# Sigmoid attention: the score slots of two pairs of heads take turns

## The reference, cut to what matters

```
x_h = layernorm(x).reshape(B, T, H, HD)                # B=2, T=1024, H=16, HD=8
Q, K, V = (x_h * sign(bv_q), x_h * sign(bv_k), x_h * sign(bv_v))
scores = einsum('bqhd,bkhd->bhqk', Q, K) * HD ** -0.5
attn = where(causal, sigmoid(scores * 4.0), 0.0)
out = einsum('bhqk,bkhd->bqhd', attn, V)
```

## Time and profile before

| what | us |
| --- | --- |
| runs: median (lowest to highest) | 1137.98 (1134.75 to 1138.6) |
| the profiled execution, its own time | 1134.96 |
| its span in the trace | 1133.0 |
| sigmoid stage in it, first score matmul to first matmul of the experts | 36.84 to 196.44 |

### The profile page before, as it was taken

How to read it: one execution, slowest core, us unless ns; L and a number is a source line. 1 busy time by engine, 2 the same in 40 slices (tenths; PEclk the granted TensorE clock), 3 DMA queues, 4 the chain that set the end, 5 groups by cost and what they waited for, 6 DMA issues and landing times. The chain is left out here.

```text
span 1133.0 us, 22305 instructions
## 1 busy us (share of the span) xinstructions
PE 1026.2 (91%) x7828; PEld 641.8 (57%) x7828; DVE 757.1 (67%) x1707; ACT 728.0 (64%) x1087; POOL 541.2 (48%) x707
## 2 busy tenths in 40 slices
PE   3899999999999469999999899999999878999997
PEld 2444444777776334555554445555444556878785
DVE  7235341777865476887788788777785257676766
ACT  1699987555546137777777677777776555545453
POOL 1377775665644122333455533344222276655564
PEclk9999999999999658999999999999999899999999
DMA  4541231536466596888888888888771574343342
GB/s 161 190 128 62 84 98 55 160 115 189 140 179 198 192 254 195 243 241 240 244 260 254 235 245 240 240 245 240 217 220 40 128 226 121 122 118 121 118 122 92
DMA packets 146430, 197.41 MB, mean 174 GB/s; under 512 B 33292, under 2 KB 113149, under 8 KB 146285
## 3 DMA queue, kind: packets, MB, share of 16 engines
q1 hardware_dynamic: 126254, 184.32, 52.4%
q0 software_dynamic: 20064, 11.66, 6.1%
HBM read 123.00 MB, written 72.74 MB: 173 GB/s over the span
## 5 line engine op out<-in xcount | busy, mean ns | idle before, releaser
L1090 DVE TENSOR_REDUCE a_part<-a_duo 128x2 f32<-128x1024 f32 (+3 forms) x256 | 215.3, 855 | 14.1 <-PE a_duo L963 12.6
L755 POOL DMA_DIRECT2D scr_y1c<-ys x240 | 118.9, 504 | 204.1 <-DVE ys L1071 201.2
L1083 DVE CUSTOM_DVE_ANT_0 a_band_sum<-a_duo,a_rel_raw 128x256 f32<-128x256 f32 (+2 forms) x320 | 131.4, 447 | 84.2 <-PE a_duo L963 64.3
L1529 POOL TENSOR_TENSOR f_hid_lo<-f_hid,att 128x512 fp32r<-128x512 f32 (+1 forms) x100 | 129.4, 1297 | 106.8 <-ACT att L1498 106.8
L976 PE MATMUL a_duo<-att 32*128 32x512 f32 (+3 forms) x672 | 139.2, 410 | 21.1 <-DVE a_part L1090 12.9
L963 PE MATMUL a_duo<-att 31*128 31x512 f32 (+3 forms) x672 | 145.4, 428 | 9.0 <-DVE a_part L1090 4.1
L706 ACT ACTIVATE a_probs<-a_duo 128x1024 f32<-128x1024 f32 x192 | 139.9, 829 | 14.1 <-PE a_duo L655 12.7
L1043 ACT ACTIVATE a_rel<-a_rel_ps 128x384 f32<-128x384 f32 x240 | 117.5, 490 | 48.3 <-PE a_rel_ps L950 47.7
L1661 DVE TENSOR_TENSOR f_hid<-f_u,w_share 128x512 f32<-128x512 f32 (+1 forms) x168 | 116.3, 692 | 27.5 <-POOL f_hid_lo L1529 4.6
L644 POOL TENSOR_TENSOR a_probs<-a_probs,const 128x256 f32<-128x256 f32 x128 | 101.5, 809 | 48.8 <-ACT a_probs L706 48.6
L1529 POOL TENSOR_TENSOR f_hid_lo<-f_hid,f_hid_hi 128x512 fp32r<-128x512 f32 x68 | 88.0, 1294 | 76.0 <-ACT f_hid_hi L1498 76.0
(11 more groups left out here) (268 smaller groups left out, 2048.1 us busy)
## 6 DMA issues: line engine op xcount, KB each, us to landing
a_rel_raw<-scr_rel SPq DMA_DIRECT2D x128, 384.0 KB, 4.5
scr_rel<-a_rel SPq DMA_DIRECT2D x120, 384.0 KB, 3.7
w_share<-scr_cw SPq DMA_DIRECT2D x144, 128.0 KB, 3.2
w_share<-scr_cw SPq DMA_DIRECT2D x44, 256.0 KB, 3.3
scr_y1c<-ys POOLq DMA_DIRECT2D x240, 8.0 KB, 3.7
w_share<-scr_cw SPq DMA_DIRECT2D x20, 192.0 KB, 2.8
w_share<-scr_cw SPq DMA_DIRECT2D x16, 224.0 KB, 3.0
att<-scr_q SPq DMA_DIRECT2D x36, 96.0 KB
```

The costliest lines, as they stand in the source:

```text
L755: eng.dma_start(scr["y1c"][w, b, head, :, at:at + T // 4], sb["ys"][32 * (2 * hd + c) + HD * w:32 * (2 * hd + c) + HD * (w + 1), h % 2, :] ...
L1083: ins = dve.tensor_tensor_reduce(band_sum[:, m % 2, hd, 0:wide], both[:, hd, (a - 4 * x) * P:(b - 4 * x) * P], rel_raw[:, e % RING, hd, (a ...
L1090: ins = dve.tensor_reduce(part[:, h % 2, x, :, j % 4], both[:, :, lo * P:hi * P], AX.X, ALU.max, negate=True)
L1529: pool.tensor_tensor(hid_lo[0:m, n % 4, :], hid[0:m, n % 2, :], f32(hid_hi[0:m, n % 4, :]), ALU.subtract).then_inc(lo_ready, 1)
```

## The change

- Two pairs of heads form a quad of 24 slots. Even slots belong to the even pair, in the order before (`EVEN`); odd slots belong to the odd pair, which goes through its lower half first (`ODD`).
- Each pair sums in a bank of its own: `acc_of(h)` is `acc[pair % 2]` for both halves. The four groups of a quad end after slots 8, 15, 23 and 24 (`ENDS`), in the order odd pair lower, even pair upper, even pair lower, odd pair upper (`GROUPS`). The first slot of a group waits for the save of the last group in its bank, `before(h)`.
- `vs` has four places in place of two, `probs` seven in place of eight (`KEPT`).
- The loads of pair 1 move from SyncE's queue at the start of the stage to ScalarE's in `prepare`, ahead of its Exp. SyncE loads the next quad's two pairs behind the third and behind the fourth group of a quad.

```
--- before.py
+++ after.py
@@ -411,6 +411,9 @@
             for c in range(NC):
                 act.wait_ge(turned, c + 1)
                 act.activation(x_hi[:, c * CH:(c + 1) * CH], bank[c][:], ACT.Copy).then_inc(hi_ready, 1)
+            act.wait_ge(ahead.qk_stored, 16 * 6)
+            for hd in range(2):
+                load_sigmoid_head(sb, scr, act, 1, hd, ahead.qk_loaded[1])
             act.wait_ge(exp_in, 1)
             act.activation(sc[:], sc[:], ACT.Exp).then_inc(exp_ready, 1)
 
@@ -515,12 +518,15 @@
     HALF, QUARTER = T // 2, T // 4
     PAIRS = B * H // 2
     K3 = TERMS * HD
-    PER = 12
-    SLOTS = PER * PAIRS
-    KEPT = 8
+    PER = 24
+    SLOTS = PER * PAIRS // 2
+    KEPT = 7
     HELD, LAG = 7, 4
     TURN, STEP = 20, 6 * P
     UPPER, LOWER = (0, 7, 1, 6, 2, 5, 3, 4), (0, 3, 1, 2)
+    EVEN, ODD = [(1, kt) for kt in UPPER] + [(0, kt) for kt in LOWER], [(0, kt) for kt in LOWER] + [(1, kt) for kt in UPPER]
+    GROUPS = ((1, 0), (0, 1), (0, 0), (1, 1))
+    ENDS = (8, 15, 23, 24)
     with ExitStack() as ctx:
         def tile(name, shape, dt=F32):
             return ctx.enter_context(nc.sbuf_tensor("a0_" + name, shape, dt))
@@ -529,7 +535,7 @@
             return ctx.enter_context(nc.semaphore("a0_" + name))
 
         qs, ks = (sb["att"][:, i, :, :] for i in range(2))
-        vs = tile("v", [P, 2, 2, NB, 32])
+        vs = tile("v", [P, 4, 2, NB, 32])
         probs = tile("probs", [P, KEPT, 2, HALF])
         ys = sb["ys"]
         duo = [ctx.enter_context(nc.psum_tensor(f"a0_duo{i}", [P, 2, HALF], F32)) for i in range(3)]
@@ -552,8 +558,8 @@
             return pair // 2 % 2
 
         def place(n):
-            pair, i = n // PER, n % PER
-            return (pair, 1, UPPER[i]) if i < NB else (pair, 0, LOWER[i - NB])
+            quad, i = n // PER, n % PER
+            return (2 * quad + i % 2, *(ODD if i % 2 else EVEN)[i // 2])
 
         def first_column(n):
             pair, x, kt = place(n)
@@ -568,10 +574,19 @@
 
         def group(n):
             pair, x, kt = place(n)
-            return 2 * pair + 1 - x
+            return 4 * (pair // 2) + GROUPS.index((pair % 2, x))
+
+        def owner(h):
+            return 2 * (h // 4) + GROUPS[h % 4][0], GROUPS[h % 4][1]
+
+        def acc_of(h):
+            return acc[owner(h)[0] % 2]
 
         def last_of(h):
-            return PER * (h // 2) + (NB, PER)[h % 2]
+            return PER * (h // 4) + ENDS[h % 4]
+
+        def before(h):
+            return max((i for i in range(h) if acc_of(i) is acc_of(h)), default=-1)
 
         block = ctx.enter_context(nc.Block())
 
@@ -581,13 +596,13 @@
                 load_sigmoid_head(sb, scr, sp, pair, hd, qk_loaded[pair % 4])
 
             def store(h, hd):
-                pair, x = h // 2, 1 - h % 2
+                pair, x = owner(h)
                 for c in range(2):
                     at = x * HALF + c * QUARTER
                     sp.dma_start(scr["y0h"][2 * pair + hd, :, at:at + QUARTER],
                                  ys[32 * (2 * hd + c):32 * (2 * hd + c) + HD, h % 2, :]).then_inc(y_stored[h % 2], 16)
 
-            for pair in range(1, 4):
+            for pair in range(2, 4):
                 for hd in range(2):
                     load(pair, hd)
             loading = weights_loaded(weights, d, sp, stage, STEP)
@@ -604,12 +619,12 @@
                 sp.wait_ge(y_saved, 2 * pair + 1)
                 for hd in range(2):
                     store(2 * pair, hd)
-                if pair + 4 < PAIRS:
-                    sp.wait_ge(st_ready, PER * (pair + 1))
-                    if pair + 4 == PAIRS // B:
+                if pair % 2 and pair + 4 < PAIRS:
+                    sp.wait_ge(st_ready, PER * (pair // 2 + 1))
+                    if pair + 3 == PAIRS // B:
                         sp.wait_ge(ahead.qk_stored, 16 * 12)
                     for hd in range(2):
-                        load(pair + 4, hd)
+                        load(pair + 3, hd)
                 if pair == 2:
                     sp.wait_ge(ahead.zeroed, 1)
                     sp.dma_start(scr["rel"][:, :, :, 0:P - 1].rearrange("s h p u -> p (s h) u"),
@@ -619,6 +634,9 @@
                 sp.wait_ge(y_saved, 2 * pair + 2)
                 for hd in range(2):
                     store(2 * pair + 1, hd)
+                if pair % 2 and pair + 4 < PAIRS:
+                    for hd in range(2):
+                        load(pair + 4, hd)
 
         @block.gpsimd
         def _(pool):
@@ -626,17 +644,17 @@
             pool.wait_ge(cleared, 1)
 
             def copy_v(pair):
-                if pair >= 2:
-                    pool.wait_ge(pv_done, PER * (pair - 1))
-                pool.tensor_copy(vs[:, pair % 2, :, :, 0:HD],
+                if pair >= 4:
+                    pool.wait_ge(pv_done, PER * (pair // 2 - 1))
+                pool.tensor_copy(vs[:, pair % 4, :, :, 0:HD],
                                  sb["v"][:, 2 * pair * NB * HD:2 * (pair + 1) * NB * HD]
                                  .rearrange("p (h j d) -> p h j d", h=2, d=HD)).then_inc(v_ready, 1)
 
-            copy_v(0)
-            copy_v(1)
+            for pair in range(4):
+                copy_v(pair)
             for n in range(SLOTS):
-                if n % PER == 6 and 2 <= n // PER + 1 < PAIRS:
-                    copy_v(n // PER + 1)
+                if n % PER in (6, 14) and 2 <= n // PER + 1 < PAIRS // 2:
+                    copy_v(2 * (n // PER) + (2 if n % PER == 6 else 3))
                 if on_diagonal(n):
                     lo = first_column(n)
                     pool.wait_ge(sig_done, n + 1)
@@ -648,7 +666,7 @@
             def scores(n):
                 pair, x, kt = place(n)
                 lo = first_column(n)
-                if n % PER == 0:
+                if n % PER < 2:
                     pe.wait_ge(qk_loaded[pair % 4], 64 * (pair // 4 + 1))
                 wait(pe, sig_done, n - 2)
                 for hd in range(2):
@@ -659,11 +677,11 @@
             def values(n):
                 pair, x, kt = place(n)
                 h = group(n)
-                if n % PER == 0:
+                if n % PER < 2:
                     pe.wait_ge(v_ready, pair + 1)
                 if kt == 0:
-                    wait(pe, y_saved, h - 1)
-                    wait(pe, router.cw_saved, min(h - 1 - TURN, NB))
+                    wait(pe, y_saved, before(h) + 1)
+                    wait(pe, router.cw_saved, min(before(h) + 1 - TURN, NB))
                 if on_diagonal(n):
                     pe.wait_ge(masked, diagonals(n + 1))
                 else:
@@ -673,7 +691,7 @@
                         lo = max(kt * P - x * HALF - c * QUARTER, 0)
                         if lo < QUARTER:
                             to = 32 * (2 * hd + c)
-                            ins = pe.matmul(acc[h % 2][to:to + 32, lo:QUARTER], vs[:, pair % 2, hd, kt, :],
+                            ins = pe.matmul(acc_of(h)[to:to + 32, lo:QUARTER], vs[:, pair % 4, hd, kt, :],
                                             probs[:, n % KEPT, hd, c * QUARTER + lo:(c + 1) * QUARTER],
                                             start=(kt == 0), stop=(kt == (4 if x else 1 + c)))
                 ins.then_inc(pv_done, 1)
@@ -684,7 +702,7 @@
                 if h == TURN:
                     pe.wait_ge(router.cw_ready, 1)
                 for i in range(2):
-                    ins = pe.transpose(acc[h % 2][0:router.layer.E + 1, QUARTER + i * P:QUARTER + (i + 1) * P],
+                    ins = pe.transpose(acc_of(h)[0:router.layer.E + 1, QUARTER + i * P:QUARTER + (i + 1) * P],
                                        router.cw[:, 2 * (h - TURN) + i, :], sb["const"][:, C_ID:C_ID + P])
                 ins.then_inc(router.cw_turned, 1)
 
@@ -735,8 +753,8 @@
                     dve.wait_ge(ahead.guarded, 16)
                     dve.wait_ge(router.cw_turned, h - TURN + 1)
                     dve.tensor_copy(sb["cwT"][0:router.layer.E + 1, at:at + 2 * P],
-                                    acc[h % 2][0:router.layer.E + 1, QUARTER:QUARTER + 2 * P]).then_inc(router.cw_saved, 1)
-                dve.tensor_copy(ys[:, h % 2, :], acc[h % 2][:, 0:QUARTER]).then_inc(y_saved, 1)
+                                    acc_of(h)[0:router.layer.E + 1, QUARTER:QUARTER + 2 * P]).then_inc(router.cw_saved, 1)
+                dve.tensor_copy(ys[:, h % 2, :], acc_of(h)[:, 0:QUARTER]).then_inc(y_saved, 1)
                 beside = choosing if h < 16 else splitting
                 next(beside, None)
                 next(beside, None)
```

37 lines of the change are left out of this document (20 added, 17 removed).

## The result

The changed kernel has a median of 1152.07 us (1149.57 to 1160.85, five runs) against 1136.66 (1134.75 to 1138.6, five runs) before: ratio 1.0144, interval 1.0103 to 1.0186. It is slower by 15.4 us; I had said 6.4 slower, with 1151 as the upper end. The direction was right, the size was not.

What follows compares the result with a forecast made beforehand. In the sigmoid stage it took TensorE and ScalarE as both close to full, ScalarE idle 1.0 a pair behind score matmuls. Terms -7.3 + 4.5 + 4.8 + 1.5 + 0.7 + 2.2 = +6.4 gave 1144 us, range 1135 to 1151.

Steps and rivals of the forecast that it cites:

- A: Sigmoid stage: alternating slots let four partition quarters overlap, ScalarE idle 1.0 a quad against 2.0; seven quads give -7.3 us.
- E: Start of the sigmoid stage: pair 1's loads from ScalarE's queue land at 39.5 and delay slot 1: +0.7 us.
- C: Group 7's copy: it waits for group 5's stores, hung behind the guard DMA, and holds slot 49's values: +4.8 us.
- D: TensorE's clock: half pace for three us behind the stall of C: +1.5 us.
- B: Quad ends: VectorE's side steps between the close third and fourth copies delay slot 25's values: +4.5 us.
- F: End of the stage: SyncE's stores and router weights finish later behind the last values, delaying the experts: +2.2 us.
- Nothing: masks: POOL's masks in the sigmoid stage: two diagonal slots in a round cost 2 x 0.73 to 0.81, adding nothing.
- late first loads: Rival, start of the stage: pair 1 lands near 44, E is 4, PE's clock starts lower: 1148 to 1151; chance 0.08.
- X: In B, the two VectorE side steps between a quad's third and fourth copies; stall X - 0.46, less about 0.2.
- Four quarters don't overlap: Rival, score matmuls: PE keeps 0.66 a score part, A falls to -5: +8.8, 1147; chance 0.10.
- Faster: Rival: group 5's stores get through before group 7 ends, C and D go: -5, 1133; chance 0.14.
- same: Rival: the stalls are there but each some 1.5 smaller: +1 to +3, 1139 to 1141; chance 0.18.

Runs made afterwards that it cites:

- e10: e7 with the change's two rows buffers and seven probabilities in place of four and six: 1138.06 us, ratio 1.0001 to the kernel before.
- e11: The changed kernel run again with no edit: 1153.37 us, ratio 1.0116 to the kernel before.
- e9: e7 with VectorE's router pieces and side steps spread over other groups: 1133.96 us, ratio 0.9972 to the kernel before.
- e1: The changed kernel with pair 1's loads issued by SyncE right behind pair 0's, not by ScalarE: 1146.13 us, ratio 1.0112 to the kernel before.
- e12: e7 with four unused VectorE copies added between the third and fourth copy of quad 3: 1141.71 us, ratio 1.0012 to the kernel before.
- e3: The changed kernel without VectorE side steps between a quad's third and fourth copy, four behind the fourth: 1150.89 us, ratio 1.0145 to the kernel before.
- e2: The changed kernel with the guard's write in eight pieces, one behind each of the first eight pairs: 1148.74 us, ratio 1.0128 to the kernel before.
- e4: The changed kernel with e1 to e3 together and the router weights' loads one pair earlier: 1147.97 us, ratio 1.0133 to the kernel before.
- e5: The changed kernel with e1, e3, earlier router weights, guard in `prepare`, four `ys` buffers, `KEPT` 6, pair and weight loads reordered: 1136.96 us, ratio 0.9999 to before.
- e6: e5 with two unused VectorE copies added between the third and fourth copy of quad 3: 1137.10 us, ratio 0.9998 to the kernel before.
- e7: e5 with the Q and K pair loads back where the change has them: 1134.57 us, ratio 0.9983 to the kernel before.

## Why the prediction was wrong

The nearest to a clean price of the order is e10's, which has the change's buffers and none of its large stalls (ScalarE still has gaps of 1.57 and 1.18 behind the close copies of quads 5 and 6). With it the 21.8 us that the quads gained in the changed kernel's first profile come apart:

| term | forecast | measured | from |
| --- | --- | --- | --- |
| A, order | -7.3 | -1.7 | quads 1 to 7, e10 less before: 131.41 - 133.09 |
| E, first loads (and the first quad) | +0.7 | +6.1 | 26.98 - 20.88 |
| C with D, guard and clock | +6.3 | +6.9 | quad 2, 25.01 - 18.14 (e10) |
| B, close copies | +4.5 | +10.5 | quads 1, 3, 5, 6 less e10's: 1.45 + 3.37 + 2.70 + 2.95 |
| F, end of the stage | +2.2 | +2.7 | 7.11 - 4.39 |
| later stages, same code | 0 | +1.5 | the span's 26.0 less the rest |

In the second profile (e11), E is 3.9, C with D 7.5 and B 6.3 (0.2 of it in quads 4 and 7), so the quads gain 15.9; with F 18.6, and its later stages took another 9.8. Both profiled executions are the slowest of their five. The terms of a run that is 15.4 slower, as the median is, are thus not known; E, C with D and B each cost some us in both profiles.

**A, mis-sized.** That four row quarters can run side by side was right, and so was the walk through a free quad: 17.6 forecast, 17.69 measured. The sign that I named for it, odd slots' score matmuls within 0.05 of the even ones, came in 9 of 31 rounds only: ScalarE set the pace. The failed step is the multiplication by seven (which gives 7.0, besides, and not 7.3). Quad by quad, e10 less before is -1.40, -0.49, +0.01, -0.93, +0.24, +0.78 and +0.10: only quads 1 and 4 had near the full gain. "Nothing: masks" took a mask at 0.73 to 0.81, a mean, as harmless; beside VectorE's side steps single ones take 1.2 and more, and in a round with two of them values come late. This is read from rows, and no run took the side steps away altogether. Quads 5 and 6, with the router pieces, were long before (19.64 and 19.98); e9 gave them 19.7 with fewer pieces in them, so what holds them there stays open.

The prediction read the Trainium skill's page "TensorE: Matmul & The Clock Gate" (Measured speedup vs the span model) as 0.15 more for four tiles than for one; the rows show 0.50 for four, where one has a mean of 0.494. The page's 3.07 is against one after another, and that fits: on the same partitions the next matmul starts 0.34 later, so four in turn would take 3 x 0.34 and 0.39 to 0.49 for the last, 1.4 to 1.5, an estimate, and 2.8 to 3.0 times 0.50.

**E, mis-sized.** I had the landing between 36.8 and 39.8; it was 42.8. The failed step is the taking over of pair 0's time from issue to landing: e1 shows that the same loads, issued as late by SyncE and with the stores behind them, hold TensorE up by 0.86 only. The rival "late first loads" had this mechanism and 1148 to 1151, the nearest of all, at a chance of 0.08. It too was short, since TensorE was still at its low pace at 50.64, where e1 was past it at 46.45, and everything up to there ran slow. In e11, with the full clock's record 4.9 earlier, E was 3.9.

**D, mis-sized, and B with it.** I counted one stall that is followed by half clock, at 1.5. e12 prices that at 2.9. The side steps' gaps summed to 6.0 where I had 4.5 (1.33 for 0.2, 1.83 for 1.1, 1.19 for 1.3, 1.62 for 1.9), and e3, in which the first three are gone, shows that they are the side steps'. The failed step is that I gave none of them a price for the clock: it fell behind three of them in the first profile and behind one in the second, for 6.8 us each, at 2.8 in quad 3 (22.0 against 19.18 in e1 and e2). B's own sum is uneven too: X - 0.66 is 1.2 for an X of 1.85 and of 1.87, and I put 1.1 and 1.3.

**C and F, right.** The hung stores, the slot they hold up and the gap of 3.98 were as forecast (3 to 5), though it came at 89 to 93 and not at 81 to 86, with the late first quad ahead of it; e2 takes it away, and e4 the end's 2.7.

**The rivals.** "Four quarters don't overlap" fell (it had A at -5 where the bound said 0). "Faster" and "same" rest on hidden stalls: the stalls were there. That the large ones can be taken out is shown by e5 to e10; even then the new order is worth no more than this measurement can tell.

## What to carry to other kernels

Price a new order on all its repetitions, not on the free one: what else runs beside it (masks, side work, a queue) differs from one to the next, and two of seven had near the full gain. When a change makes engines arrive earlier or closer together, go through the one DMA queue in its order of issue: each large or late transfer there becomes a stall, and mending one passes the gain on to the next (e3, e4) until all the large ones are out of the way (e5 to e10). A stall of 4.3 us cost 7.2. And profile a kernel twice before a price is put on a single stall: the same stall was followed by half clock in one execution and not in another.

## What the hardware showed that I had not expected

- Four 24-row score matmuls of 512 columns in four row quarters took 0.50 us together, two after two 0.73.
- What TensorE's idle time was followed by, at a granted clock of 0.50: 3.86 us (e12, ScalarE's gap of 4.30) by 10.2 us; 1.60 by 6.8 in the changed kernel and in e11, by none in e1, e2 and e6; 1.39 to 1.41 by 6.8, 3.4 or none; 1.82 by 6.8 in the changed kernel and by none in e1; 0.91 and 0.96 in e4 by 3.4 each.
- A GpSimd mask of 128x256 took 0.73 us with VectorE idle or copying out of `acc`, and 1.20 beside a 128x512 VectorE operation (e7, at 103.63).
- Pair 1's four loads, issued by ScalarE from 27.2 us beside SyncE's stores, landed 15.6 us later, at 42.8; issued by SyncE behind pair 0's and ahead of the stores, and done with the issues at the same time, they held TensorE up by 0.86 us only.
